# The memory layer: another order of TensorE's work within a slot

## The reference, cut to what matters

```python
def step(carry, inp):                      # over the W = 32 segments
    mem, z = carry
    q_s, k_s, v_s, qn_s, kn_s = inp        # with rope, and without (qn, kn)
    scores = einsum('bhnd,bhmd->bhnm', q_s, k_s) * SCALE
    sdpa = einsum('bhnm,bhmd->bhnd', softmax(where(mask, scores, -inf)), v_s)
    sq = elu1(qn_s)
    mem_out = einsum('bhnk,bhkv->bhnv', sq, mem) / (einsum('bhnk,bhk->bhn', sq, z)[..., None] + 1e-06)
    out = beta * mem_out + (1.0 - beta) * sdpa
    sk = elu1(kn_s)
    prev_v = einsum('bhnk,bhkv->bhnv', sk, mem) / einsum('bhnk,bhk->bhn', sk, z)[..., None]
    mem = mem + einsum('bhnk,bhnv->bhkv', sk, v_s - prev_v)
    z = z + sk.sum(axis=2)
    return ((mem, z), out)
```

## Time and profile before

| | |
|---|---|
| median of 3 runs | 3136.75 us (3122.73 to 3139.36) |
| the profiled execution | 3142.25 us, span 3140.3 us |
| granted TensorE clock, whole span | 0.843 of full |
| busy, whole span | TensorE 80%, VectorE 57%, ScalarE 45%, GpSimd 30% |
| memory layer's slots | 2039.4 to about 2966 us of the span |

### The profile page before, as it was taken

One profiled execution on the slowest core, in us unless ns is written; L12 is line 12 of the kernel. 1 busy time (PEld: TensorE's weight loads), 2 busy tenths in 40 slices (PEclk: granted clock), 3 DMA queues, 4 the chain that ended last, 5 costly groups with the idle time before them and its releaser, 6 DMA issues. The chain is left out here.

```text
span 3140.3 us, 83029 instructions
## 1 busy us (share of the span) xinstructions
PE 2508.0 (80%) x32464; PEld 1920.3 (61%) x32464; DVE 1776.3 (57%) x5798; ACT 1423.9 (45%) x3433; POOL 932.0 (30%) x936
## 2 busy tenths in 40 slices
PE   2359967779933899998998969488898889898777
PEld 1239964559921444444444449387887878787677
DVE  3453346543345655665655433377787778777633
ACT  1236653256621444454544536244444444444354
POOL 0006650036630000000000006255454545454345
PEclk9559987669965988898988969699899999998778
DMA  3001120001154111110110001200000000000012
GB/s 111 0 29 47 48 81 3 27 24 48 47 173 119 26 27 31 30 39 20 48 27 22 2 30 47 80 3 3 3 3 3 4 4 3 3 4 3 29 29 86
DMA packets 61331, 107.37 MB, mean 34 GB/s; under 512 B 14420, under 2 KB 33533, under 8 KB 58526
## 3 DMA queue, kind: packets, MB, share of 16 engines
q1 hardware_dynamic: 47134, 73.82, 7.8%
q0 software_dynamic: 13824, 28.34, 3.2%
HBM read 70.74 MB, written 35.18 MB: 34 GB/s over the span
## 5 line engine op out<-in xcount | busy, mean ns | idle before, releaser
L1211 ACT ACTIVATE ca_pt<-ca_ps 128x512 f32<-128x512 f32 (+3 forms) x768 | 352.9, 491 | 417.8 <-PE ca_ps L1298 278.1
L568 PE MATMUL ffn_ps<-ffn_xst,ffn_up_w 128*128 128x128 f32 x3456 | 430.2, 279 | 0.2 <-issue 0.2
L568 PEld LDWEIGHTS ffn_ps<-ffn_xst,ffn_up_w 128*128 128x128 f32 x3456 | 412.0, 195 | 1.2 <-issue 1.2
L409 POOL MEMSET ffn_later<- 128x128 f32 x4 | 0.8, 206 | 1231.2 <-POOLq L42 1231.2
L682 DVE TENSOR_TENSOR ffn_hid<-ffn_sg,ffn_ps 128x512 f32<-128x512 f32 x216 | 148.6, 688 | 363.1 <-PE ffn_ps L568 361.7
L1410 DVE TENSOR_REDUCE ca_m_far<-ca_ps 128x1 f32<-128x128 f32 (+5 forms) x384 | 238.9, 622 | 162.2 <-PE ca_ps L1274 158.4
L1651 ACT ACTIVATE im_pe_<-im_s,im_nm 128x32 f32<-128x32 f32 x512 | 158.1, 310 | 320.2 <-DVE im_nm L1809 320.2
L1609 POOL TENSOR_TENSOR im_rope_qk<-im_t 128x512 f32<-128x512 f32 x128 | 202.5, 1582 | 284.5 <-DVE im_t L1790 280.7
L440 POOL DMA_INDIRECT ffn_xs<-ffn_x,ffn_token_at x216 | 209.1, 968 | 257.2 <-DVE ffn_token_at L665 192.6
L1274 PE MATMUL ca_ps<-ca_stacks 72*128 72x512 bf16 (+3 forms) x768 | 233.0, 371 | 61.2 <-DMA ca_stacks<-scratch_piece 38.2
L1294 PE MATMUL ca_ps<-ca_stacks 75*128 75x512 bf16 (+3 forms) x768 | 258.0, 355 | 6.6 <-ACT ca_pt L1211 3.7
(11 more groups left out here) (316 smaller groups left out, 5177.1 us busy)
## 6 DMA issues: line engine op xcount, KB each, us to landing
ca_stacks<-scratch_piece SPq DMA_DIRECT2D x96, 192.0 KB
ffn_got<-ffn_y SPq DMA_DIRECT2D x48, 256.0 KB, 5.8
ffn_x<-ffn_xn SPq DMA_DIRECT2D x32, 256.0 KB, 2.0
scratch_piece<-ca_piece SPq DMA_DIRECT2D x24, 256.0 KB, 2.9
w_w<-in_L_ffn_experts_w_dram SPq DMA_DIRECT2D x2, 2048.0 KB, 12.7
scratch_toeplitz<-scratch_bias SPq DMA_DIRECT2D x2, 2048.0 KB, 14.4
ffn_xs<-ffn_x,ffn_token_at POOLq DMA_INDIRECT x216, 2.6
ffn_y<-ffn_ys,ffn_result_at POOLq DMA_INDIRECT x216, 2.3
```

What stands on the lines that cost most here:

```text
L568: last = nc.tensor.matmul(ps[:, bank, j * P:j * P + P], up_w[:, n % WS, first + j * P:first + j * P + P], xst[:, n % 2, :], start=True, st ...
L1211: nc.scalar.activation(pt[:, i % 8, lo - c0:hi - c0], ps[:, tile_bank(i), lo - c0:hi - c0], ACT.Exp, scale=SCALE).then_inc(p_ready, 1)
```

## The change

`project` is cut into its two halves (i = 0 for queries, 1 for keys) and `recall` into its three groups (0 scores, 1 prev, 2 num). TensorE no longer calls `walk` but has a loop of its own with the parts in another order: lift, scores, first half of the projections, prev, second half, learn, num, weigh, and turn or add as before. The waits go with the parts: `ab_used` stands ahead of the first half, `rope_ready` and `m1_ready` ahead of the scores, `el_ready` and `mem_ready` ahead of prev. `proj_ready` is signalled behind the second half, `recalled` behind num. The other engines are unchanged.

```diff
--- before.py
+++ after.py
@@ -1674,17 +1674,18 @@
                             last = nc.tensor.transpose(b_lift[:, QH * D + n * P:QH * D + n * P + P], el[:, (k - 1) % 2, PB + n, :], g.ident[:])
                     last.then_inc(S["lift_ready"], 1)
 
-                def project(k):
+                def project(k, i):
+
                     q = k % NQ
-                    if k:
+                    if k and i == 0:
                         pe.wait_ge(S["ab_used"], k)
                     x = XT[:, k // NQ, :]
-                    for i in range(2):
-                        for n in range(PB):
-                            c = (i * PB + n) * P
-                            nc.tensor.matmul(b_a[:, c:c + P], w4[:, 2 * i, q * PB + n, :], x, start=True, stop=True)
-                            last = nc.tensor.matmul(b_s[:, c:c + P], w4[:, 2 * i + 1, q * PB + n, :], x, start=True, stop=True)
-                    last.then_inc(S["proj_ready"], 1)
+                    for n in range(PB):
+                        c = (i * PB + n) * P
+                        nc.tensor.matmul(b_a[:, c:c + P], w4[:, 2 * i, q * PB + n, :], x, start=True, stop=True)
+                        last = nc.tensor.matmul(b_s[:, c:c + P], w4[:, 2 * i + 1, q * PB + n, :], x, start=True, stop=True)
+                    if i:
+                        last.then_inc(S["proj_ready"], 1)
 
                 def for_heads(fn):
 
@@ -1716,20 +1717,22 @@
                                                         start=True, stop=True, skip_group_check=True)
                     last.then_inc(S["upd_ready"], 1)
 
-                def recall(j):
+                def recall(j, part):
                     q, r = j % NQ, j % 2
-                    pe.wait_ge(S["el_ready"], j + 1)
-                    pe.wait_ge(S["rope_ready"], j + 1)
-                    if j:
-                        pe.wait_ge(S["m1_ready"], j)
-                    if j >= NQ:
-                        pe.wait_ge(S["mem_ready"], j - NQ + 1)
+                    if part == 0:
+                        pe.wait_ge(S["rope_ready"], j + 1)
+                        if j:
+                            pe.wait_ge(S["m1_ready"], j)
+                    if part == 1:
+                        pe.wait_ge(S["el_ready"], j + 1)
+                        if j >= NQ:
+                            pe.wait_ge(S["mem_ready"], j - NQ + 1)
                     score = lambda half, bank, blk, b, tok: nc.tensor.matmul(ps[tok, bank, SC + blk * SEG:SC + blk * SEG + SEG], rope_qk[half, r, blk, tok], rope_qk[half, r, PB + blk, tok], start=True, stop=True, skip_group_check=True)
                     prev = lambda half, bank, blk, b, tok: nc.tensor.matmul(ps[tok, bank, PR + blk * E1:PR + blk * E1 + E1], el[half, r, PB + blk, tok], mem[half, q, b, blk, :], start=True, stop=True, skip_group_check=True)
                     num = lambda half, bank, blk, b, tok: nc.tensor.matmul(ps[tok, bank, NU + blk * E1:NU + blk * E1 + E1], el[half, r, blk, tok], mem[half, q, b, blk, :], start=True, stop=True, skip_group_check=True)
-                    for_heads(score)
-                    for_heads(prev)
-                    for_heads(num).then_inc(S["recalled"], 1)
+                    last = for_heads((score, prev, num)[part])
+                    if part == 2:
+                        last.then_inc(S["recalled"], 1)
 
                 def weigh(j):
                     pe.wait_ge(S["pte_ready"], j + 1)
@@ -1762,7 +1765,29 @@
                         last = nc.tensor.transpose(b_a[:, n * P:n * P + P], norm.xn[:, n, :], g.ident[:])
                     last.then_inc(S["turned"], 1)
                 pe.wait_ge(S["xt_ready"], 2 * BATCH)
-                walk(lift=lift_in, project=project, learn=learn, recall=recall, weigh=weigh, turn=turn, add=add)
+                for k in range(N + 4):
+                    w, slot = k // NQ, k % NQ
+                    past, now = 0 <= k - 1 < N, k < N
+                    if k <= N:
+                        lift_in(k)
+                    if past:
+                        recall(k - 1, 0)
+                    if now:
+                        project(k, 0)
+                    if past:
+                        recall(k - 1, 1)
+                    if now:
+                        project(k, 1)
+                    if 0 <= k - 2 < N:
+                        learn(k - 2)
+                    if past:
+                        recall(k - 1, 2)
+                    if 0 <= k - 2 < N:
+                        weigh(k - 2)
+                    if slot == 2 and w:
+                        turn(w, k)
+                    if slot == 3 and w:
+                        add(w, k)
 
             @block.vector
             def _(dve):
```

## The result

The changed kernel takes 3273.16 us (median of 4 runs, 3259.12 to 3306.37) against 3132.6 us (the kernel before, with a fourth run): 1.047 times the time before, with a 95% interval of 1.038 to 1.055. The forecast was slower, 3217 us, with a range to 3252. The sign and the cause held; the size did not.

The account below looks back on a forecast made before the run. TensorE and VectorE were both near full in the memory layer, with TensorE's stops disturbing. 127 slots of 7.45 us, add, tile ends, clock and stops made +80 us on 3142.25, 3217 us at the runs' median; range 3150 to 3252.

Parts of the forecast that it names:

- The ring: Memory layer: moved `m1_ready` wait closes a loop, L1822's signal through scores, projections and VectorE's queue back to L1822; 7.45 us.
- Its length in the changed kernel: Memory layer's loop per slot: 7.08 us from the rows plus 0.37 for changes of product size; bounds 7.08 and 7.51.
- The signal: In the loop, from the end of VectorE's signalling step to TensorE's start: 0.11 us.
- The changes of shape: TensorE switching between small and full-size products, three times in the loop: 0.43 us by the rows, 0.37 taken.
- Turn and add: Memory layer: turn fits the loop's idle time; add costs 0.25 us each fourth slot, 8 us; tile ends 4 us.
- The stops: TensorE's "issue" stops behind the burst, 69.6 us in front of num and weigh: most go, three stay, 5 us; bounds 0, 35.
- The clock: TensorE idling lowers its clock in ten of the layer's 64 plain slots, 15 us; bounds 0 and 48 us.
- the parts lie between: TensorE's idle parts, 1.5 and 0.5 us, against stops of 0.52 us (clock stays high) and 1.51 us (it doesn't).
- The range: Whole kernel, 8 in 10: 3150 to 3252 us, taking in rival 1's upper end and all of rival 4.
- Rival 3: Memory layer: clock falls in most plain slots, 64 run projections slow, 96 us less 15 counted; 3298 us, chance 0.08.
- Rivals 1, 2 and 4: Shape changes free, 3132 to 3155 us, chance 0.13; wait already satisfied, 3000 us, 0.04; stops stay, 3247 us, 0.10.
- The skill's rule: TensorE's instruction fetch: 16 KiB blocks fetched ahead and hidden by issue; by it the spread burst would win nothing.

Follow-up runs that it names:

- the one with mem's wait: Changed kernel with one half of the projections ahead of the scores and their wait, prev behind the second half; ratio 0.994 to the kernel before.
- L1822 early: Changed kernel with VectorE's step that makes uu moved behind the one that reads num; ratio 1.031 to the kernel before.
- wait filled: Changed kernel with five unread full-size products (1.1 us) added in front of the scores' wait in half of the slots; ratio 1.029 to the kernel before.
- the two profiles: Profiled executions of the changed kernel, first comparison and unchanged rerun on another chip; ratios 1.047 and 1.044, first to last lift 1019.3 and 1043.3 us.

## Why the prediction was right about the cause and wrong about the size

- *The ring*, right. The rings of the six experiments that have one were forecast from the same parts and came within 0.05 us, but the one with mem's wait (6.41 for 6.1). The totals did worse: of these six only L1822 early and wait filled came within the range I gave, as ratios.
- *Its length in the changed kernel*, 7.45 forecast, 7.56 measured, 0.05 over my upper bound. The signal took 0.15 us, not 0.11. The changes of shape cost 0.45 us: TensorE's part is 2.97 us for 2.52 us of work (0.24, 0.29 and 1.99). The rows gave 0.43, and I took 0.37. (The new order has four more changes per slot, six in place of two, not five as I wrote; three stand in the loop, so the sum is untouched.) 127 times 0.11 is 14 us.
- *Turn and add.* The slot behind an add is 7.90 us, 0.34 over the ring, not 0.25: 3 us more. VectorE's work at a tile's end costs 0.53 us seven times, as forecast.
- *The stops*, right: of 69.6 us 6.8 remain. They cost the ring some 7 us where I had put 5: in 13 slots the updates stop and VectorE's mem waits for them.
- *The clock*, the step that failed. I took ten slow slots at 1.5 us, 15 us in all. There are 15 and 29 in the two profiles, and each costs 1.95 us on average, since the scores and prev between the halves run slowly as well: 29 and 56 us. I took the price from a slot of before in which only the projections stood behind the slow clock's start, and the number from no row at all: that "the parts lie between" 0.52 and 1.51 us says nothing of how many fall. The runs give it only in part: with 0.25 us of idling in front of the scores no plain slot is slow, with 1.01 us 25 are, with 1.37 us 15 and 29.
- *The range.* My bounds allowed 48 us for the clock, 35 for the stops and 7.51 us for the ring; together they reach past 3280. I drew the end at 3252 by adding parts of them, and even those parts (7.51, 30 and 20) add up to 3255, not to the 3249 that I wrote.
- *Where the 56 us are.* The lifts should have taken 976 us. In the first profile they take 43 more: 14 from the ring, 3 from the add, 14 from slow plain slots, some 7 from the layer's first five slots, which are slow too, 2 from the stops, the rest small. In the second they take 67 more, 41 of them from slow plain slots. The median lies 56 us over the forecast, between the two; no profile shows its own parts.
- *Rival 3* had the mechanism, at a third to a little over half of its price: 15 and 29 of some 64 plain slots, 29 and 56 us for its 96. Its sign, a granted clock under 0.85 in the layer, was not met (0.95 and 0.91). Rivals 1, 2 and 4 were seen not to happen: the wait is there, the stops are gone, and the changes of shape cost what the rows said.
- *The skill's rule* that instruction fetch is mostly hidden (Trainium skill, "Runtime: NRT & Kernel Launch", Instruction fetch mechanics) does not fit this burst, if the stops are fetches, as their spacing and the packets suggest: 69.6 us of stops go to 18.3 when the burst is thinned, with more instructions to fetch, not fewer. If they are, what counts here is the pace of the burst.

## What to carry to other kernels

When work is interleaved to smooth one engine, write down the waits that move with it, and walk the ring that each closes: the slot can't be shorter than signal, own part and the other engine's queue up to the signal. The same wait was long satisfied at the end of this slot and set its length at the head; with half of the projections and the updates ahead of the wait, and the reading of num earlier on VectorE, the same interleaving went from 4.4% slower to 1.7% faster. And price a low clock by the slot in which it will fall, with all that then stands in the ring, not by its share of the stage.

## What the runs showed of the hardware

Giving TensorE 1.1 us of useless products in front of a 1.37 us wait made the kernel 1.5% faster: the projections behind came back to 278 ns from means of 294 and 307, and the granted clock of the layer to 0.99 from 0.95 and 0.91. Idling of 1.01 us in each plain slot was enough for slow projections in 25 of them. And where a dense burst of 256 small instructions was issued in 1.5 us, TensorE stopped 37 times in the layer, for 1.9 us each; the layer's 38 stops of over 1 us lie whole numbers of 256 TensorE instructions apart, to within one. With 192 in a row behind full-size work 9 to 24 us of stops were left in the whole layer, with 128 6.8 us.
